# F and O gates with stationary weights in an LSTM with residual

## The reference

```python
xW = jnp.einsum('ntd,dk->tnk', x, Wx) + b
c0 = jnp.zeros_like(h0)
def step(carry, xw_t):
    prev_h, prev_c = carry
    a = xw_t + prev_h @ Wh
    i = jax.nn.sigmoid(a[:, 0:Hdim])
    f = jax.nn.sigmoid(a[:, Hdim:2 * Hdim])
    o = jax.nn.sigmoid(a[:, 2 * Hdim:3 * Hdim])
    g = jnp.tanh(a[:, 3 * Hdim:4 * Hdim])
    next_c = f * prev_c + i * g
    next_h = o * jnp.tanh(next_c)
    return ((next_h, next_c), next_h)
```

## Time and profile before

| | |
|---|---|
| median of 3 runs | 1062.12 us (1061.99 to 1062.6) |
| profiled execution | 1062.23 us, its span 1060.4 us |
| TensorE matmuls busy | 867.7 us (82%), 37888 of them |
| TensorE weight loads busy | 635.6 us (60%) |
| VectorE busy | 784.5 us (74%) |
| ScalarE busy | 548.2 us (52%) |

### The profile page before, as it was taken

How to read it: one execution, slowest core, us unless ns; L and a number is a source line. 1 busy time by engine, 2 the same in 40 slices (tenths; PEclk the granted TensorE clock), 3 DMA queues, 4 the chain that set the end, 5 groups by cost and what they waited for, 6 DMA issues and landing times.

```text
span 1060.4 us, 90187 instructions
## 1 busy us (share of the span) xinstructions
PE 867.7 (82%) x37888; PEld 635.6 (60%) x37888; DVE 784.5 (74%) x4899; ACT 548.2 (52%) x3586; POOL 0.7 (0%) x6
## 2 busy tenths in 40 slices
PE   4888888888888888888888888888888888888886
PEld 3666656656666666556566666665665666666654
DVE  5777777777777777777777777777777777777776
ACT  2555555555555555555555555555555555555554
POOL 0000000000000000000000000000000000000000
PEclk9999999999999999999999999999999999999999
DMA  3000000000000000000000000000000000000000
GB/s 91 6 7 6 6 6 6 7 6 6 7 6 6 7 6 6 6 6 7 6 6 7 6 6 6 6 6 6 6 7 6 6 7 6 6 6 6 6 6 7
DMA packets 32110, 8.74 MB, mean 8 GB/s; under 512 B 31584, under 2 KB 31584, under 8 KB 32096
## 3 DMA queue, kind: packets, MB, share of 16 engines
q1 hardware_dynamic: 31488, 8.41, 3.6%
q10 hardware_dynamic: 608, 0.14, 0.1%
HBM read 6.43 MB, written 2.10 MB: 8 GB/s over the span
## 4 chain that ended last, share of the span: by engine, by line
DVE 52%; PE 23%; ACT 15%; issue 8%; SPq 1%; DVEq 1%; DMA 0%
DVE turned_bank L299 40%; PE gates L372 23%; ACT tanh_o L213 8%; DVE h_pad L317 8%; ACT turned_bank L216 6%; DVE scan_both L304 3%; DVEq L333 1%; SPq L140 1%; DVE h_rows L273 0%; DMA wh_raw<-in_L_cond_Wh_dram 0%; SPq L144 0%; PE x_acc L364 0%; PE gates L358 0%; DVEq L272 0%; DVE wh L226 0%
## 5 line engine op out<-in xcount | busy, mean ns | idle before, releaser
L372 PE MATMUL gates<-wh,h_pad 128*32 128x64 f32 x32768 | 565.0, 221 | 175.7 <-DVE h_pad L317 174.2
L372 PEld LDWEIGHTS gates<-wh,h_pad 128*32 128x32 f32 x32768 | 482.6, 110 | 356.3 <-DVE h_pad L317 354.3
L299 DVE STREAM_TRANSPOSE turned_bank<-gates 128x64 f32<-128x64 f32 x2048 | 475.3, 263 | 163.3 <-PE gates L372 153.8
L204 ACT ACTIVATE tanh_f<-turned_bank 128x8 f32<-128x8 f32 x512 | 90.7, 177 | 431.1 <-DVE turned_bank L299 390.5
L364 PE MATMUL x_acc<-wh,zeros 128*32 128x256 f32 x1024 | 305.0, 379 | 0.3 <-issue 0.3
L349 PE MATMUL x_acc<-wx,x_units 128*32 128x128 f32 x2048 | 203.6, 284 | 9.4 <-DVE x_units L252 9.4
L211 ACT ACTIVATE scan_both<-turned_bank 128x8 f32<-128x8 f32 x1024 | 185.1, 181 | 48.5 <-DVE turned_bank L299 1.7
L317 DVE SCALAR_TENSOR_TENSOR h_pad<-tanh_o,turned_bank 128x4 f32<-128x4 f32 x1024 | 133.0, 158 | 73.3 <-ACT turned_bank L216 0.4
L310 DVE TENSOR_TENSOR_SCAN cell<-scan_both 128x12 f32<-128x12 f32 x1024 | 145.2, 182 | 0.0
L216 ACT ACTIVATE turned_bank<-cell 128x4 f32<-128x4 f32 x1024 | 143.7, 173 | 0.0
L349 PEld LDWEIGHTS x_acc<-wx,x_units 128*32 128x32 f32 x2048 | 94.9, 109 | 51.8 <-issue 9.3
(11 more groups left out here) (28 smaller groups left out, 9.1 us busy)
## 6 DMA issues: line engine op xcount, KB each, us to landing
x_next<-in_x_dram SPq DMA_DIRECT2D x256, 8.0 KB
x_here<-in_x_dram SPq DMA_DIRECT2D x256, 8.0 KB
out_dram<-y_rows SPq DMA_DIRECT2D x256, 8.0 KB
wx_raw<-in_L_cond_Wx_dram SPq DMA_DIRECT2D x8, 128.0 KB, 3.4
wh_raw<-in_L_cond_Wh_dram SPq DMA_DIRECT2D x8, 128.0 KB, 2.8
bias_raw<-in_L_cond_b_dram ACTq DMA_DIRECT2D x4, 32.0 KB, 3.0
h_rows<-in_cond_dram ACTq DMA_DIRECT2D x4, 1.0 KB
```

The lines of the kernel that those rows point to most:

```text
L299: nc.vector.transpose(turned[k], gates[k][:, 0:W]).then_inc(gates_turned[k], 1)
L372: last = nc.tensor.matmul(gates[k][q * R:(q + 1) * R, 0:W], h_stationary(b, t), wh[:, b, q, columns_of(k)], start=False, stop=b == M - 1, ...
```

## The change

The diff is cut to its core; the reordering of the names of the banks and the semaphores is left out.

- I and G stay by rows in BA and BB. F and O are computed by units: the weights are the stationary operand (32 columns for F, by `units`), and the four columns of the hidden state move. Their results land as units by step and batch in `f_units[m]` and `o_units[m]`, and need no transpose.
- O uses tiles of 64 columns (`o_part`) with a copy of its weights, `wh_o`, whose columns stand block by block: two calls for each b and m.
- The x part of F and O is transposed once per chunk (`turn_x_part`) and injected by units. F is injected with the rows at the end of step 7, O at step 0 (`inject_o`).
- VectorE's order is BA, forget(0), BB, update(0), forget(1), update(1), hidden(0), hidden(1). The forget product and its tanh are split by m. BB is transposed into SBUF, and the tanh of the cell of m=1 lies in SBUF.
- The x product is made in two sets of four calls of 256 columns, at steps 4 and 5, where `keep_busy` is left out; the bias is added at step 6, the transpose at step 7.

```diff
-    BF, BA, BB, BO = range(4)
+    BA, BB, BF, BO = range(4)
+    ROWS = (BA, BB)
-    FIRST_PIECE_AT = 3
+    X_PRODUCT_AT = (4, 5)
+    X_PART_AT = STEPS - 2
+    UNIT_COLUMNS = slice(GC - 4 * R, GC)
...
+        a_bank = ps("a_bank", [128, 512])
+        turned = {BA: a_bank[:, 0:W], BB: sb("turned_b", [128, W])[:]}
+        tanh_c = [a_bank[:, W:W + N], sb("tanh_c1", [128, N])[:]]
...
-                    act.wait_ge(gates_turned[BF], now)
-                    nc.scalar.activation(tanh_f[:], of_step(BF, t), ACT.Tanh).then_inc(tanh_f_done, 1)
                     for m in range(M):
+                        act.wait_ge(f_done[m], now)
+                        nc.scalar.activation(tanh_f[:, m, :], f_units[m][:, t * N:(t + 1) * N], ACT.Tanh).then_inc(tanh_f_done[m], 1)
                         act.wait_ge(gates_turned[AB[m]], now)
...
-                    act.wait_ge(gates_turned[BO], now)
-                    nc.scalar.activation(tanh_o[:], of_step(BO, t), ACT.Tanh)
                     for m in range(M):
+                        act.wait_ge(o_done[m], now)
+                        nc.scalar.activation(tanh_o[:, m, :], o_units[m][:, t * N:(t + 1) * N], ACT.Tanh).then_inc(o_tanh_done, 1)
                         act.wait_ge(cell_done[m], now)
...
+            def make_wh_o(b):
+                return nc.vector.tensor_scalar(wh_o[:, b, :, :].rearrange("p m (q r) -> p q m r", q=Q),
+                                               wh_raw[:, b, O * D:(O + 1) * D].rearrange("p (q m r) -> p q m r", q=Q, m=M),
+                                               0.25, None, ALU.mult)
...
+            def turn_x_part(chunk):
+                dve.wait_ge(x_part_made, chunk + 1)
+                nc.vector.transpose(x_part_units[:], x_part[:, UNIT_COLUMNS]).then_inc(x_part_turned, 1)
...
-                if ahead and t == STEPS - 1:
+                if ahead and t == X_PART_AT:
                     make_x_part(chunk + 1)
+                if ahead and t == X_PART_AT + 1:
+                    turn_x_part(chunk + 1)
...
-                turn(BF)
                 turn(BA)
+                forget(0)
                 turn(BB)
-                forget()
-                turn(BO)
                 update(0)
+                forget(1)
                 update(1)
...
+            def inject_o(m):
+                at = BO * W + m * R - UNIT_COLUMNS.start
+                for p in range(Q // 2):
+                    nc.tensor.matmul(o_units[m][p * 2 * R:(p + 1) * 2 * R, 0:R], ident[:, p * 2 * R:(p + 1) * 2 * R],
+                                     x_part_units[:, at:at + R], start=True, stop=False,
+                                     tile_position=(0, p * 2 * R), skip_group_check=True)
+
+            def inject_early():
+                for k in ROWS:
+                    inject(k)
+                for m in range(M):
+                    inject_units(f_units[m], BF, m)
...
+                def units(b, bank, k, m):
+                    at = k * W + m * R
+                    for q in range(Q):
+                        last = nc.tensor.matmul(bank[q * R:(q + 1) * R, t * N:(t + 1) * N], wh[:, b, q, at:at + R],
+                                                h_at(b, t - 1), start=False, stop=b == M - 1,
+                                                tile_position=(0, q * R), skip_group_check=True)
+                    return last
+
+                def o_part(b, m):
+                    for p in range(Q // 2):
+                        last = nc.tensor.matmul(o_units[m][p * 2 * R:(p + 1) * 2 * R, t * N:(t + 1) * N],
+                                                wh_o[:, b, m, p * 2 * R:(p + 1) * 2 * R],
+                                                h_at(b, t - 1), start=False, stop=b == M - 1,
+                                                tile_position=(0, p * 2 * R), skip_group_check=True)
+                    return last
+
                 pe.wait_ge(h_done[0], now)
-                recur(0, BF)
+                rows(0, BA)
+                units(0, f_units[0], BF, 0)
+                rows(0, BB)
                 pe.wait_ge(h_done[1], now)
-                recur(1, BF).then_inc(gates_done[BF], 1)
-                for k in (BA, BB, BO):
-                    recur(0, k)
-                    recur(1, k).then_inc(gates_done[k], 1)
-                if t < STEPS - 1 or not ahead:
+                rows(1, BA).then_inc(gates_done[BA], 1)
+                units(1, f_units[0], BF, 0).then_inc(f_done[0], 1)
+                rows(1, BB).then_inc(gates_done[BB], 1)
+                units(0, f_units[1], BF, 1)
+                units(1, f_units[1], BF, 1).then_inc(f_done[1], 1)
+                if t == 0:
+                    for m in range(M):
+                        inject_o(m)
+                for m in range(M):
+                    o_part(0, m)
+                    o_part(1, m).then_inc(o_done[m], 1)
+                if ahead and t in X_PRODUCT_AT:
+                    x_product(X_PRODUCT_AT.index(t), chunk + 1)
+                elif ahead and t == X_PART_AT:
+                    pe.wait_ge(x_part_made, chunk + 2)
                     keep_busy()
-                if t == STEPS - 1 and ahead:
-                    pe.wait_ge(x_part_made, chunk + 2)
-                    for k in BANKS:
+                elif t < STEPS - 1 or not ahead:
+                    keep_busy()
+                if ahead and t == STEPS - 1:
+                    for k in ROWS:
                         pe.wait_ge(gates_turned[k], now)
-                        inject(k)
+                    for m in range(M):
+                        pe.wait_ge(tanh_f_done[m], now)
+                    pe.wait_ge(x_part_turned, chunk + 2)
+                    inject_early()
                     keep_busy()
```

More of the change, by code:

```diff
@@ L53, in lstm_residual_kernel @@
         wh = sb("wh", [128, M, Q, GC])
+        wh_o = sb("wh_o", [128, M, M, Q * R])
         bias_raw = sb("bias_raw", [128, NG, QD])
@@ L63, in lstm_residual_kernel @@
         x_part = sb("x_part", [128, GC])
+        x_part_units = sb("x_part_units", [128, UNIT_COLUMNS.stop - UNIT_COLUMNS.start])
         tanh_f = sb("tanh_f", [128, M, N])
@@ L342, in _, with x_product @@
         def _(pe):
-            def x_product(b, columns, chunk):
-                opens = (b, columns) == PIECES[0]
-                if opens:
+            def x_product(b, chunk):
+                if b == 0:
                     pe.wait_ge(x_turned, chunk + 1)
                 for q in range(Q):
-                    last = nc.tensor.matmul(x_acc[q * R:(q + 1) * R, columns], x_units[:, b * R:(b + 1) * R],
-                                            wx[:, b, q, columns], start=opens, stop=b == M - 1,
+                    last = nc.tensor.matmul(x_acc[q * R:(q + 1) * R, 0:GC], x_units[:, b * R:(b + 1) * R],
+                                            wx[:, b, q, :], start=b == 0, stop=b == M - 1,
                                             tile_position=(0, q * R), skip_group_check=True)
-                if (b, columns) == PIECES[-1]:
+                if b == M - 1:
                     last.then_inc(x_acc_done, 1)
@@ L368, in step, with rows @@
                 now = chunk * STEPS + (t + 1)
-                def recur(b, k):
+                def rows(b, k, columns=slice(0, W)):
                     for q in range(Q):
-                        last = nc.tensor.matmul(gates[k][q * R:(q + 1) * R, 0:W], h_stationary(b, t),
-                                                wh[:, b, q, columns_of(k)], start=False, stop=b == M - 1,
+                        last = nc.tensor.matmul(gates[k][q * R:(q + 1) * R, columns], h_stationary(b, t),
+                                                wh[:, b, q, k * W + columns.start:k * W + columns.stop],
+                                                start=False, stop=b == M - 1,
@@ L391, in step @@
                     keep_busy()
-                if ahead and 0 <= t - FIRST_PIECE_AT < len(PIECES):
-                    x_product(*PIECES[t - FIRST_PIECE_AT], chunk + 1)
             pe.wait_ge(zeroed, 2)
             pe.wait_ge(wx_made, M)
-            for piece in PIECES:
-                x_product(*piece, 0)
+            for b in range(M):
+                x_product(b, 0)
             pe.wait_ge(ident_made, 1)
             pe.wait_ge(zeroed, 2)
-            pe.wait_ge(x_part_made, 1)
-            for k in BANKS:
-                inject(k)
@@ L404, in _ @@
-            pe.wait_ge(wh_made, M)
+            pe.wait_ge(x_part_turned, 1)
+            inject_early()
+            pe.wait_ge(wh_made, 2 * M)
             with pe.Fori(0, CHUNKS - 1) as k:
```

42 lines of the change are left out of this document (26 added, 16 removed).

## The result

The changed kernel is slower. Four runs took 1088.68, 1090.51, 1107.84 and 1117.55 us, against 1062.05 us (median of four) for the kernel before. The forecast was 1000 us, with a range of 962 to 1066. The profiled execution is the one of 1088.68 us, span 1086.7 us. The page first: busy us with share and instructions, then the chain that ended last (rows 1 and 2 of before).

What follows compares the result with a forecast made beforehand. The prediction took a ring of hand-overs, run 512 times, to bound the kernel: 511 x 1.88 = 960.7, plus 9.5 step 7, 4 irregular steps, 24.9 head, tail and launch, 0.3 start-up: 999.4, so 1000 us, range 962 to 1066.

Steps and rivals of the forecast that it cites:

- What bounds the kernel: Whole kernel: no engine is full; time is 512 times a ring of hand-overs, a plain step now 2.02 us.
- m=1's road: Plain step, through forget(1), the scan, tanh and hidden product of m=1: closes at 1.87 to 1.90 us.
- TensorE's passes: TensorE, each step: F's unit pass 0.028 us, bounded by its weight load; O's pass of 64 weight columns 0.055.
- the sum: TensorE's own work per step: rows 0.45, F 0.22, O 0.44, zeros 0.43, together 1.54 us, under the ring.
- The rival of narrow passes at 0.056: TensorE's unit passes: no quicker than now, both roads 0.11 later, step 1.99, 1056 us; chance 12%.
- the drain rival: TensorE's tile switches: each empties the array, 0.17 to 0.22 us; step 1.96, 1041 us; chance 13%.
- The new ring: Plain step after the change: roads by m=0 and m=1 both close at 1.88 us, 0.14 less than now.
- the 4 us of irregular steps: Whole run: allowance for irregular steps, some 5 us before, carried with 4 us (0 to 7).
- Step 7: Chunk border: injection and zeros end near 2.07, tile 0 0.15 us late once a chunk, 9.5 us in all.
- The clock: TensorE's clock, rival: falls to the lower level; a third of the steps low gives 1150 us; chance 13%.
- The code: TensorE's loop, 354 calls: stays loaded; rival: reload stops 0.59 us in each chunk, 37 us, 1037 us, chance 6%.

Runs made afterwards that it cites:

- the two edits that shortened m=1's road: Changed kernel with tanh of the cell (1) in PSUM, m=0's in SBUF: 1084.25 us; changed kernel with F's second half ahead of A's: 1081.9 us.
- Loops of 354 and 378 calls: 354: the changed kernel, 1088.68 us at best; 378: changed kernel with each step's zeros call repeated on the three other tiles, 1104.21 us.
- of 418 and 424: 418: changed kernel with O in 32-column tiles, 1508.95 us; 424: kernel before with two banks' passes issued as two 32-column calls, 2012.47 us.
- the two versions that touched the long call behind step 7's injection: Changed kernel with cell in PSUM, F first, waits one by one; step 7's zeros left out: 1671.79 us, or spread over four tiles: 1687.04 us.

## Why the prediction was wrong

*What bounds the kernel: right.* It is a ring of hand-overs before and after; the two edits that shortened m=1's road by some 0.04 moved the step by 0.033 and 0.044.

*TensorE's passes: the unit passes right, the sum too small.* F's pass takes 0.028 and O's 0.058, as chosen (0.028, 0.055); four-column matmuls take 169 to 173 ns. The rival of narrow passes at 0.056 is refuted. The switch to 64-column tiles costs 0.12 and the one back for the zeros 0.13, less than the 0.17 to 0.22 that the drain rival took. Counted as in the sum, 0.216 after the start of their second matmul, the zeros end 0.10 before the next step instead of 0.3. The Trainium skill, TensorEngine Tiling (Array Packing), Key Properties, says that a change of tiling mode drains TensorE. The trace agrees in so far as the gap is gone with 32-column tiles; it lies beside the ring and costs nothing in a plain step.

*The new ring: this is the step that failed.* The text has m=1's road close at 1.87 to 1.90. From TensorE's start on h of m=1 to the next such point the forecast has 2.165 - 0.28 = 1.885, and the trace 2.408 - 0.379 = 2.029. The road that closes it runs F(0), tanh, forget(0), transpose BB, tanh of I,G(1), update(1), tanh of the cell (1), hidden(1). Measured from transpose BA, the same time after h as forecast (0.39), the lateness builds up:
- tanh of F(0) starts 0.09 after it, not 0.03: +0.06. The end of a matmul is seen by ScalarE 0.12 later, not the 0.07 taken over from VectorE. The text bounded it at 0.10 and said that it was worth at most 0.04.
- transpose BB follows forget(0) by 0.08, not 0.05, but ends sooner (0.24 for 0.26): tanh of I,G(1) is still at +0.06.
- That tanh reads SBUF and takes 212 ns, not 181. update(1) then waits for it by a wait instruction of its own, and starts 0.10 after the tanh's end, not 0.03. With these two this hand-over overtakes forget(1), from which the text let update(1) start: update(1) is at +0.10. (update(0) has the same 0.10 behind tanh of I,G(0), and is 0.07 late by it.)
- tanh of the cell (1) writes SBUF, 207 ns for the 180 of the sum: +0.04 with its hand-over. The tanh_c line of the diff was read and not priced.

Together 0.14 in that road. The plain step is 2.029 for 1.88, and 511 times the difference is 76 of the 89 us between 1000 and 1088.7. To these come 10.1 for the first chunk, 3.7 more than forecast at the borders, 2.9 for the last chunk and 0.8 at head and tail; the 4 us of irregular steps did not come.

*Step 7: the place was right, the cause half.* The text took 0.15 late for the zeros on tile 0, 9.5 us in all; the border costs 0.22, 13.2 us. The trace shows the loop's branch behind the injection, which makes the first load of step 0 0.16 late. No row of before showed this cost, since there the branch (1.641) and its 0.36 ended just ahead of h (2.017). Tile 0's lateness is real too: in the changed kernel the first eight loads of step 0 start within 0.16, not 0.05, and first load to hidden(0) takes 1.898, where the version with zeros on all four tiles, whose branch is later still, takes 1.777.

*The clock: named, and sized as if all or nothing.* In its mild form it cost 9 us in the profiled execution, which had one low chunk at the start, and the slowest of the four runs took 29 more, about what 24 further low steps cost. The earlier trace rows had shown that the run begins low, and the sum carried no such term. In the variants that took filler columns from TensorE, or spread them, it became the rival in full: 1369, 1672 and 1687 us.

*The code: right that it stays loaded.* Loops of 354 and 378 calls do, of 418 and 424 don't. The Trainium skill, Runtime: NRT & Kernel Launch, Instruction fetch mechanics, gives TensorE room for 2048 instructions. Each fp32 call is two loads and two matmuls, so by an estimate 378 calls are 1512 and 418 are 1672, beside the waits and the loop's own: counted so, the limit found here is lower than that figure. The rival's price, 0.59 a chunk, was far too small: 2.9 and 7.5 us a chunk. What the text missed is the last chunk with its three stops.

What stays open: why the low level lasts one chunk in one execution and four in another, and what the fetching of code has to do with the stops of the last chunk. That the low level ends just behind step 7, and never ended in the two versions that touched the long call behind step 7's injection, points at that step; which part of it counts wasn't settled.

## What to carry to other kernels

When a change splits one wide step into two interleaved halves, follow both roads to the end with every in-order neighbour on each engine, and price a new hand-over (here TensorE to ScalarE) or another memory for an operand by its own bounds on each of them; here the second road closed the ring. A kernel whose TensorE is "98% busy" with filler isn't bound by it: look at what its weight loads wait for. Before taking columns off TensorE, try the kernel with less filler: half of each zeros' call less cost the kernel before nothing and the changed one 270 us (1369 against 1099, medians of four).

## What the runs showed of the hardware

- A pass of four fp32 matmuls with 32-column weights and four moving columns takes 0.028 us, with 64-column weights 0.058; switching between the tilings 0.12 and 0.13 (changed kernel against the version with O in 32-column tiles).
- ScalarE's tanh of 4 elements read from SBUF takes 171 ns into PSUM and 207 into SBUF (178 and 198 with the two exchanged). Read from PSUM into SBUF it takes 155 to 173. Of 8 elements into SBUF it takes 181 ns from PSUM and 212 from SBUF.
- From the end of the last matmul to the tanh that waits for it 0.12 us pass, to VectorE's transpose 0.07. From the end of a tanh to a scan that stands behind a wait instruction of its own it is 0.10.
- On TensorE the next weight load comes 0.36 to 0.39 us after the start of a loop's branch, and the branch waits its turn behind the queued calls, filler too.
- TensorE can be busy all the time at the low clock for 90 us, and at the low clock for the whole run in two versions (zeros' mean 635 ns), while a kernel with 74% busy matmuls of 64 and 128 columns keeps the high one.
